# Summing the gathered expert rows on TensorE, with the later layer's maps prepared beside the gathers, in a two-layer transformer kernel on one core

## The reference, cut to what matters

```python
eo = einsum('eci,eih->ech', hid, down_proj) * buf_w[..., None]
routed = zeros((T + 1, h)).at[buf_tok.reshape(-1)].add(eo.reshape(-1, h))[:T]   # six weighted rows for each token
```

## Time and profile before

| | us |
|---|---|
| median of 3 runs | 786.45 (785.43 to 788.97) |
| the profiled execution's own time | 787.34 |
| its span | 785.7 |
| fold stage begins | 515.8 |
| first copy of a turned u (L1890) | 616.47 |

### The profile page before, as it was taken

The page is one execution under the profiler, slowest core; times in us unless marked ns, Lnnn a source line. Parts: engine busy times, 40 slices in busy tenths (PEclk is TensorE's granted clock), DMA queues, the critical chain, the costliest instruction groups (busy, mean ns, idle before and its releaser), DMA issues. The chain is left out here.

```text
span 785.7 us, 10359 instructions
## 1 busy us (share of the span) xinstructions
PE 577.7 (74%) x3486; PEld 368.9 (47%) x3486; DVE 389.2 (50%) x1102; ACT 233.4 (30%) x638; POOL 295.2 (38%) x383
## 2 busy tenths in 40 slices
PE   2666259970799999998953398984336697897796
PEld 1334125530466666665632254564213586554485
DVE  4656213333475676855442033366758547624135
ACT  1222024440132232321310144420033463142664
POOL 0556611106601537160326012257754266003065
PEclk9757569995799999998985599987577798998899
DMA  8886048842200314340166168733370000000001
GB/s 322 290 295 215 16 129 271 282 164 80 73 9 1 81 41 85 35 170 4 37 241 138 55 211 301 243 104 98 89 80 1 0 1 1 1 1 0 2 1 53
DMA packets 39723, 82.96 MB, mean 106 GB/s; under 512 B 7805, under 2 KB 27906, under 8 KB 38816
## 3 DMA queue, kind: packets, MB, share of 16 engines
q1 hardware_dynamic: 26144, 45.03, 17.7%
q0 software_dynamic: 13248, 37.07, 17.2%
q10 hardware_dynamic: 288, 0.30, 0.1%
HBM read 60.21 MB, written 26.35 MB: 110 GB/s over the span
## 5 line engine op out<-in xcount | busy, mean ns | idle before, releaser
L434 POOL DMA_INDIRECT expert_in<-xn_sent,scatter_slots x72 | 70.9, 985 | 79.7 <-DVE slots L383 50.5
L770 DVE SCALAR_TENSOR_TENSOR work<-work,banks 128x96 f32<-128x96 f32 x64 | 16.3, 254 | 124.1 <-ACT work L750 124.1
L1845 PE MATMUL banks<-w_gu,w_dn 128*128 128x256 f32 x256 | 68.4, 394 | 0.0
L1610 POOL DMA_INDIRECT w_dn<-expert_out,slots x48 | 51.3, 1069 | 26.4 <-issue 14.2
L790 PE MATMUL banks<-ident,work 128*128 128x128 f32 x128 | 29.5, 316 | 42.6 <-DMA work<-expert_in 42.6
L1251 POOL DMA_INDIRECT w_gu<-expert_out,gather_slots x48 | 49.3, 1028 | 28.7 <-DVE gather_slots L1259 14.7
L799 PE MATMUL banks<-w_gu,work 128*64 128x192 f32 x512 | 58.5, 352 | 0.0
L1968 POOL TENSOR_TENSOR var_eps<-mv,eps 128x1 f32<-128x1 f32 (+1 forms) x70 | 13.7, 195 | 116.8 <-ACT w_dn L1894 55.2
L1845 PEld LDWEIGHTS banks<-w_gu,w_dn 128*128 128x128 f32 x256 | 46.0, 199 | 4.2
L790 PEld LDWEIGHTS banks<-ident,work 128*128 128x128 f32 x128 | 13.8, 149 | 67.5 <-issue 41.5
L1970 POOL TENSOR_TENSOR rstd<-var_eps,minus_half 128x1 f32<-128x1 f32 (+1 forms) x70 | 42.4, 606 | 5.5
(11 more groups left out here) (271 smaller groups left out, 1258.0 us busy)
## 6 DMA issues: line engine op xcount, KB each, us to landing
work<-expert_in SPq DMA_DIRECT2D x64, 128.0 KB, 3.8
expert_out<-work SPq DMA_DIRECT2D x64, 128.0 KB, 3.8
w_gu<-in_gate_up SPq DMA_DIRECT2D x10, 768.0 KB
w_gu<-in_gate_up POOLq DMA_DIRECT2D x6, 768.0 KB, 5.6
expert_in<-w_dn SPq DMA_DIRECT2D x4, 1024.0 KB, 7.5
w_dn<-in_down SPq DMA_DIRECT2D x10, 384.0 KB
w_gu<-in_gate_up SPq DMA_DIRECT2D x1, 3840.0 KB, 12.0
w_dn<-in_down SPq DMA_DIRECT2D x1, 3072.0 KB, 25.8
```

What stands on the lines that cost most here:

```text
L434: nc.gpsimd.indirect_dma_start(out=m.expert_in, out_offset=bass.IndirectOffsetOnAxis(m.scatter_slots[u][:, at:at + 1], 0), in_=xn[:, t, :] ...
L1610: nc.gpsimd.indirect_dma_start(out=w.combined[q % 2][:, t * TOPK + k, :], out_offset=None, in_=m.expert_out, in_offset=bass.IndirectOffset ...
L1845: last = nc.tensor.matmul(f.p_lin[t % DEEP], f.uT[t % DEEP][:, c, :], w.lin[:, step, c, :], start=(step > 0 and c == 0), stop=(c == KC - 1))
```

## The change

The fold stage and the last stage become one block. The phases' reduction goes to GpSimd, ahead of its weight loads in the second expert stage. The gathered rows are summed by TensorE: ScalarE scales the identity by a column of weights, and six products of such a diagonal with a gathered tile are accumulated; VectorE adds the sum to x. Each tile has a place of its own for its six rows (the last one uses the first one's). `finish_maps` runs before the first norm's statistics; qkv maps come after those of tiles 4 and 5. The first norm goes in groups of tiles 0 to 3, 4 and 5, 6 and 7; the sines of tiles 0 to 3 follow their own Tanh. The diff, cut:

```diff
         if call == 1:
             @block.gpsimd
             def _(pool):
-
+                phases_to_turns(nc, m, a, pool, x.out, before)
...
+def phases_to_turns(nc, m, a, pool, s_out, before):
...
+    pool.dma_start(w.phase, a["rows"][:, first:first + NL * PW * D].broadcast_to([P, NL * PW * D])).then_inc(m.s_phase, 16)
+    pool.dma_start(w.ent_b.rearrange("p a b -> p (a b)"), a["ent_b"]).then_inc(m.s_phase, 16)
+    pool.wait_ge(m.s_phase, 32)
...
+    for l in range(NL):
+        phase, turns, whole = w.phase[:, l * PW * D:(l + 1) * PW * D], w.turns[l], w.cos_turns[l]
+        chain(nc.gpsimd.tensor_scalar(turns, phase, 0.5 / PI, big, ALU.mult, ALU.add))
+        chain(nc.gpsimd.tensor_scalar(whole, turns, -big, None, ALU.add))
+        for part in (c1, c2):
+            chain(nc.gpsimd.tensor_scalar(turns, whole, -part, None, ALU.mult))
+            chain(nc.gpsimd.tensor_tensor(phase, phase, turns, ALU.add))
+        chain(nc.gpsimd.tensor_scalar(turns, phase, TURN_PI, -TURN_PI, ALU.min, ALU.max))
+    pool.wait_ge(s_out, before + RING)
+    for l in range(NL):
+        chain(nc.gpsimd.tensor_copy(w.ent_b_wide[:, l], w.ent_b[:, l, :].unsqueeze(2).broadcast_to([P, EW // P, P])))
...
+def fold_pool(nc, m, w, s, wave, pool):
+    last_row = pool.to_reg(SLOTS + P - 1)
+    for t in range(TILES):
+        if t == 6:
+            pool.wait_ge(s.sin, 2 * NL)
+        if t == 7:
+            pool.wait_ge(s.summed, 1)
+        for k in range(TOPK):
+            nc.gpsimd.indirect_dma_start(
...
+        if t == 5:
+            norm_roots_pool(nc, m, wave, pool, 0, [0])
+        if t == 6:
+            norm_roots_pool(nc, m, wave, pool, 0, [1])
+    norm_roots_pool(nc, m, wave, pool, 0, [2])
...
+    def diagonals(t):
+        for k in range(TOPK):
+            j = t * TOPK + k
...
+            nc.scalar.activation(w.diag[j % DIAGS], m.ident[:, :], ACT.Copy, scale=m.weights[:, t, k:k + 1]
+                                 ).then_inc(s.diag, 1)
+
+    for l in range(NL):
+        nc.scalar.activation(w.cos_turns[l], w.turns[l], ACT.Abs).then_inc(s.abs, 1)
...
+    for t in range(5):
+        diagonals(t)
+    wave_scalar_x(nc, w, f, wave, act, 0, range(0, 4))
+    wave_scalar_sines(nc, w, f, wave, act, 0, range(0, 4))
+    diagonals(5)
+    wave_scalar_x(nc, w, f, wave, act, 0, range(4, 6))
+    diagonals(6)
+    diagonals(7)
+    wave_scalar_x(nc, w, f, wave, act, 0, range(6, 8))
...
+    def add_sum(t):
+        dve.wait_ge(s.summed, t + 1)
+        chain(nc.vector.tensor_tensor(m.x[:, t, :], m.x[:, t, :], m.banks[:, 2 + t % 2, 0:D], ALU.add))
+        dve.sem_inc(s.added, 1)
...
+    add_sum(0)
+    add_sum(1)
...
+    finish_maps(nc, m, w, dve, chain, s.maps, s.scaled, s.last_steps, lambda: (add_sum(2), add_sum(3)))
+    stats_all_vector(nc, m, wave, chain, range(0, 4))
+    apply_all_vector(nc, m, f, wave, dve, 0, range(0, 4))
+    add_sum(4)
+    add_sum(5)
+    stats_all_vector(nc, m, wave, chain, range(4, 6))
+    dve.wait_ge(s.small, 4 * 16)
+    finish_qkv(nc, w, chain)
+    apply_all_vector(nc, m, f, wave, dve, 0, range(4, 6))
+    wave_vector_u(nc, f, wave, dve, 0, range(0, 4))
+    for t in range(6, 8):
+        add_sum(t)
+        stats_all_vector(nc, m, wave, chain, range(t, t + 1))
+    apply_all_vector(nc, m, f, wave, dve, 0, range(6, 8))
...
+    def sum_tile(t):
+        if t >= 1:
+            pe.wait_ge(s.added, t)
+        for k in range(TOPK):
+            j = t * TOPK + k
+            if k == 0:
+                pe.wait_ge(s.gathered[t], 16 * TOPK)
+            pe.wait_ge(s.diag, j + 1)
+            last = nc.tensor.matmul(m.banks[:, 2 + t % 2, 0:D], w.diag[j % DIAGS], w.combined[t][:, k, :],
+                                    start=(k == 0), stop=(k == TOPK - 1))
+            last.then_inc(s.used if k < TOPK - 1 else s.summed, 1)
...
+    sum_tile(0)
+    sum_tile(1)
+    for k in range(1, STEPS):
+        step_shift(k)
+    sum_tile(2)
+    sum_tile(3)
+    pe.wait_ge(s.scaled, 1)
...
+    sum_tile(4)
+    wave_tensor_x(nc, m, w, f, wave, pe, 0, range(0, 4), f.p_turn_x)
+    sum_tile(5)
+    wave_tensor_x(nc, m, w, f, wave, pe, 0, range(4, 6), f.p_turn_x)
+    sum_tile(6)
+    sum_tile(7)
+    wave_tensor_x(nc, m, w, f, wave, pe, 0, range(6, 8), f.p_turn_x)
...
+FIRST_NORM = ((0, 4), (4, 6), (6, 8))
+OTHER_NORMS = ((0, 4), (4, 8))
```

More of the change, by code:

```diff
@@ new lines, with __init__ @@
+class Fold:
+    def __init__(self, sem):
+        self.small = sem("small_last_weights_loaded")
+        self.prod, self.read = sem("fold_product_ready"), sem("fold_products_read")
+        self.wide = sem("bias_columns_spread")
+        self.halved, self.last = sem("amplitude_map_halved"), sem("last_row_of_input_maps_ready")
+        self.abs, self.sin, self.half = sem("phase_sizes_ready"), sem("phase_sines_ready"), sem("half_pi_made")
+        self.gathered = [sem(f"last_rows_gathered_tile{t}") for t in range(TILES)]
+        self.diag, self.used = sem("weight_diagonal_ready"), sem("weight_diagonal_used")
+        self.summed, self.added = sem("tile_summed"), sem("tile_sum_added")
+        self.maps, self.scaled, self.last_steps = sem("step_maps_ready"), sem("step_maps_scaled"), sem("last_row_of_step_maps_ready")
@@ L1886, in wave_scalar, with wave_vector_u @@
                              ).then_inc(s.sines, 1)
+def wave_vector_u(nc, f, s, eng, ffn, tiles):
+    for t in tiles:
+        eng.wait_ge(s.sines, ffn * TILES + (t + 1))
+        nc.vector.scalar_tensor_tensor(out=f.u[:, t, :], in0=f.z[:, t, 0:D], scalar=1.0, in1=f.z[:, t, D:2 * D],
+                                       op0=ALU.add, op1=ALU.mult).then_inc(s.u, 1)
+def wave_scalar(nc, m, w, f, s, eng, ffn):
+    if ffn:
+        wave_scalar_x(nc, w, f, s, eng, ffn, range(TILES), f.p_turn)
+    wave_scalar_sines(nc, w, f, s, eng, ffn, range(TILES) if ffn else range(4, TILES))
     def copy_u(n, t):
@@ L2027, in _ @@
         def _(dve):
-            dve.wait_ge(w.s_small, 4 * 16)
             chain = Chain(dve, v_chain)
-            wave_vector(nc, m, w, f, wave, dve, chain, 0,
-                        meanwhile=lambda chain: finish_maps(nc, m, w, dve, chain, s_maps, s_scaled, s_last), tiles=REST)
+            fold_vector(nc, m, w, f, fold, wave, dve, chain)
+            wave_vector(nc, m, w, f, wave, dve, chain, 0)
             dve.wait_ge(s_pad, 3)
@@ L2044, in _ @@
         def _(pe):
-            def last_rows():
-                pe.wait_ge(s_scaled, 1)
-                pe.wait_ge(wave.tanh, TILES)
-                for k in range(1, STEPS):
-                    nc.tensor.matmul(m.banks[:, 4 + k, 0:D], w.last_row, w.lin[:, k, KC - 1, :], start=True, stop=True
-                                     ).then_inc(s_last, 1)
-            wave_tensor(nc, m, w, f, wave, pe, 0, s_maps, REST, last_rows)
+            fold_tensor(nc, m, w, f, fold, wave, pe)
+            wave_tensor(nc, m, w, f, wave, pe, 0, fold.maps)
             for t in range(TILES):
```

363 lines of the change are left out of this document (163 added, 200 removed).

## The result

| | before | after |
|---|---|---|
| median, us (all runs of that comparison) | 787.71 (785.43 to 789.34) | 801.0 (796.87 to 804.51) |
| ratio after to before, 95% interval | | 1.0165 (1.0126 to 1.0205) |
| the profiled execution: time and span, us | 787.34; 785.7 | 798.93; 797.2 |
| second expert stage, first row load to the fold's first VectorE operation | 441.61 to 515.99: 74.4 | 442.72 to 523.82: 81.1 |
| fold, from there to the first copy of a turned u | to 616.47: 100.5 | to 628.51: 104.7 |

The 11.5 us between the spans are 1.1 ahead of the expert stage, 6.7 in it, 4.2 in the fold and -0.5 behind. The ratios leave out executions more than 1.5% above the fastest of the same kernel; where an experiment's executions fall in two groups, the text gives all of them, since the groups are the effect.

What follows compares the result with a forecast made beforehand. Bound: gathers to 588.7 us, then 21 us of mostly VectorE work. The fold's +7.2 and the expert stage's +0.3 make +7.5 on the profiled 787.34: 794.8, or 794 in terms of the runs' median; range 782 to 800.

Steps and rivals of the forecast that it cites:

- The sign and the mechanism of the fold: Fold: slower, as GpSimd's second root waits for tile 5's sum and holds tile 7's gathers; slower given 0.66.
- First root: Fold, GpSimd's root for tiles 0 to 3: starts at 568.4 us, against 566.3 before.
- Second root: Fold, root of tiles 4 and 5: done at 593.9 us, after GpSimd has stood still for some 15 us.
- Tile 7: Fold: its gathers land at 605.3 us; its sum starts at 606.9, after tile 6's sum, and ends at 609.6.
- The no-wait rival: Fold: tile 5's sum is there when GpSimd arrives at 577.8; 6.5 us less than before, about 780; chance 0.11.
- Last products: Fold, TensorE's two products of the last wave: between 3.6 us warm and 7.2 cold, taken as 5.4.
- the fold's sum: Fold: first copy of u at 623.7 us against 616.47 before, +7.2 us.
- The expert stage: Second expert stage: late, bunched weight loads make TensorE wait for rows, between 0 and +3 us, taken as +0.3.
- The bound on GpSimd's work: Second expert stage: fourteen operations at up to 1.13 us and two at 2.26 make at most 20.3 us.
- the expert stage pays as well: Rival, expert stage: bunched loads or held VectorE add 3 to 8 us, 797 to 802; chance 0.09.
- VectorE held by GpSimd: Second expert stage: GpSimd's operations could hold VectorE for at most 8 us, at least nothing; taken as nothing.
- The table loads: Fold, ScalarE: a Sin load of 1.29 us counted without drain; the skill page's drain would add 1.4, total 795.4.

Runs made afterwards that it cites:

- the run with tile 5 early: The changed kernel with tile 5's diagonals on ScalarE and its sum on TensorE ahead of the first wave: 786.56 us, ratio to before 1.0003.
- the run with products: The kernel before plus the fourteen phase operations, loads nearly on time, and five extra TensorE products in each of pairs 12 to 20: 792.24 us.
- operations alone: The kernel before plus the fourteen GpSimd phase operations in the second expert stage, loads nearly on time, no early phase load: 792.65 us over twelve executions.

## Why the prediction was right and wrong

The sign and the mechanism of the fold were right; the median, 801.0, lies outside 782 to 800. It misses by 1.0 us, with single executions from 796.87 to 804.51, so which side of the bound it fell on was chance; that 7 to 9 us came from a place where 0.3 had been put was not.

**First root.** Forecast 52.5 us after the fold's begin (568.4 - 515.9), measured 51.8.

**Second root.** An idle of some 15 us, forecast for the order on ScalarE; 14.51 measured. Within it the wave was shorter (apply 577.02 to the last Abs 588.64, 11.6 instead of 12.5), the six diagonals took 1.84, the sum of tile 5 came at the lower clock level as assumed, 5.46 against 5.4.

**Tile 7.** "Sum of tile 7 thus starts at 606.9", set by tile 6's sum and not by the gathers (605.3): so it was, and the run with early gathers showed it. The no-wait rival got its condition in the run with tile 5 early, and its fold: 8 us below the kernel before, against the 6.5 below that it gave.

**Last products.** Taken between warm and cold, 5.4; measured 3.70, with the granted clock at 1.00 over 610 to 625. That was luck of the execution: with the same two sums ahead of them they took 5.34 in the run with early gathers and 5.40 in the change with spaced loads. With the first root and the wave this makes the fold +4.2 instead of +7.2. Three other runs with this fold took 105.1, 105.8 and 106.5 us, 4.6 to 6.0 over before: the fold's sum was too high by 1 to 3 us.

**The expert stage** is the step that failed: "between 0 and +3, I take +0.3, since the following loads have gaps to catch up in". It took 6.7 us more in the profile, and the medians leave 7 to 9 (13.3 less the fold's 4.2 to 6.0). The bound on GpSimd's work, 20.3 us, held (448.51 to 468.33, 19.8 us), though not in its parts: the fourteen operations took up to 1.53 us each instead of 1.13, the two copies 1.07 instead of 2.26. The premise held as well: the first load came 7.7 us late, the next close behind it, and the row waits grew by 1.8 us only. What the term left out is the state that TensorE can be in behind such waits: they were priced by their length, and the time came from the clock behind them, at 0.68, 0.50 and 0.80 from 480 to 495. The sum looked at TensorE's clock in the fold alone, where it was expected to be low. The rival "the expert stage pays as well" named the right place, with 797 to 802, and the condition (not done by 465: it was 468.3); it was given 0.09. Of its two mechanisms, held VectorE did not occur, and bunched loads did, but it priced them by their waits as well.

**VectorE held by GpSimd** was taken as nothing, and was. The copy that VectorE makes for each pair, before (groups: line, engine, operation, count, busy us, mean ns):

```profile
L778 DVE COPY work<-banks 96x128 f32<-96x128 f32 x29 | 8.1, 280 | 0.0
```

and after, with GpSimd's operations beside it:

```profile
L778 DVE COPY work<-banks 96x128 f32<-96x128 f32 x25 | 7.0, 280 | 0.0
```

280 ns in both, and also over 448 to 468 alone, where GpSimd's operations stand. The Trainium skill, "SBUF — State Buffer", section "Who interferes with whom", says that a VectorE instruction with at most one input from the on-chip buffer, outside the 2-port modes, does not contend with GpSimd. The trace agrees with it: the copy's only input is an accumulator bank.

**The table loads.** A load of 1.28 us starts 0.01 us behind the last Abs and the first sine 0.01 us behind the load (587.74 + 0.90, 588.65, 589.94): no gap beyond it, as taken. The drain of about 1.38 us that the Trainium skill, "ScalarE: Activation LUTs", section "What ACT_TABLE_LOAD costs", adds to a switch does not show here; the measurement decides.

**What stays open.** How the fourteen operations, with loads that were 1.4 us late at most, bring TensorE as often to the lower clock as loads that are up to three pairs late; that was not taken apart further. One thing that its trace shows: SyncE's issue of a row load took up to 1.16 us beside GpSimd's operations, against 0.43 at that place before; but the run with products has one of 1.23, and its clock stayed up. Open as well is what decides, of two executions with like gaps, which one falls. And the change with spaced loads stands 3 us higher than its fold explains, two of its executions more than that; their time was not placed.

## What to carry to other kernels

Price a stall on TensorE by what it does to the granted clock behind it as well as by its length: look at the clock's column of the windows behind each group of waits, and run often enough to see two groups. Work put on an idle DMA-issuing engine was not free here, where it delayed transfers and even where it hardly did; look at what waits for those transfers, and pace them anew. And when an engine idles before a wait, change what it waits for before moving what stands behind it: the order written for ScalarE was worth 12 us here, the order on the engine that showed the idle nothing.

## What was not expected of the hardware

An engine that is busy 5.00 us of 5 at the 1.2 GHz level did 21 to 25 matmul records in the expert stage, against 37 to 43 at 2.4 GHz, and stayed so for about 10 us (kernel after) to 24 us (operations alone) of nearly continuous work; identical code, that of the operations alone, took 785.6 in one execution and 804.9 in another. On GpSimd a 128x512 tensor-scalar operation took 0.61 to 0.62 us with two arithmetic steps in it and 1.49 to 1.53 with one (L1539 and L1544 against L1540 and L1542); the tensor-tensor sum took 1.27. Why the single step is slower was not tried.
